# Attention kernel: row scores take every eighth query, and one transfer moves the row maxima into place

## The reference

```python
qkv = jnp.einsum('oc,bchw->bohw', w_qkv, x)          # x is (8, 384, 32, 32)
q, k, v = (to_heads(t) for t in jnp.split(qkv, 3, axis=1))
att = jnp.einsum('bhxd,bhyd->bhxy', q * scale, k)
att = jax.nn.softmax(att, axis=-1)
out = jnp.einsum('bhxy,bhyd->bhxd', att, v)
out = jnp.einsum('oc,bchw->bohw', w_proj, out_as_image) + b_proj[None, :, None, None]
```

## Time and profile before

| | before |
|---|---|
| time, median of 3 runs | 4934.52 us (4933.33 to 4936.31) |
| time of the profiled execution | 4934.93 us |
| its span, first to last instruction | 4933.3 us |
| mean granted clock of TensorE | 0.960 |
| PE busy | 4420.9 us (90%), 14579 matmuls |
| PEld busy | 2648.6 us (54%) |
| DVE busy | 3114.3 us (63%) |
| ACT busy | 2416.2 us (49%) |
| POOL busy | 1192.6 us (24%) |

### The profile page before, as it was taken

One profiled execution on the slowest core, in us unless ns is written; L12 is line 12 of the kernel. 1 busy time (PEld: TensorE's weight loads), 2 busy tenths in 40 slices (PEclk: granted clock), 3 DMA queues, 4 the chain that ended last, 5 costly groups with the idle time before them and its releaser, 6 DMA issues. The chain is left out here.

```text
span 4933.3 us, 48107 instructions
## 1 busy us (share of the span) xinstructions
PE 4420.9 (90%) x14579; PEld 2648.6 (54%) x14579; DVE 3114.3 (63%) x3139; ACT 2416.2 (49%) x3705; POOL 1192.6 (24%) x920
## 2 busy tenths in 40 slices
PE   5999999999999999848999999499399999999999
PEld 4666666666666767623444443388234444444444
DVE  4656666666666666656555554333487788678767
ACT  3757675858585757532222222112154455445544
POOL 2656565555555656400000000111000000000000
PEclk8999999999999999979999999799699999999999
DMA  2010101010101111020011000324200000000000
GB/s 49 21 51 20 50 20 50 20 50 21 47 24 38 33 38 33 28 100 13 39 54 49 39 26 26 103 82 129 109 26 38 38 0 38 38 38 0 38 38 13
DMA packets 62414, 205.55 MB, mean 42 GB/s; under 512 B 32016, under 2 KB 33680, under 8 KB 52496
## 3 DMA queue, kind: packets, MB, share of 16 engines
q1 hardware_dynamic: 56944, 191.90, 11.4%
q0 software_dynamic: 3840, 11.01, 1.0%
q10 hardware_dynamic: 1440, 0.16, 0.0%
HBM read 133.95 MB, written 51.27 MB: 38 GB/s over the span
## 5 line engine op out<-in xcount | busy, mean ns | idle before, releaser
L456 POOL TENSOR_TENSOR probs_lo<-probs,probs_hi 128x512 fp32r<-128x512 f32 x840 | 1116.3, 1351 | 900.7 <-ACT probs L511 889.5
L510 ACT ACTIVATE probs_hi<-s_psum 128x512 fp32r<-128x512 f32 x1024 | 619.0, 605 | 302.7 <-PE s_psum L734 282.9
L2237 PE MATMUL psum<-mixes,conv_t 128*128 128x512 f32 x1728 | 751.1, 592 | 0.0
L581 DVE TENSOR_REDUCE maxima<-m_psum 128x1 fp32r<-128x1024 f32 x520 | 632.1, 1223 | 90.6 <-PE m_psum L712 73.6
L511 ACT ACTIVATE probs<-s_psum 128x512 f32<-128x512 f32 x1024 | 617.9, 603 | 0.0
L2237 PEld LDWEIGHTS psum<-mixes,conv_t 128*128 128x128 f32 x1728 | 327.5, 190 | 409.8 <-issue 409.8
L733 PE MATMUL s_psum<-q_all,k_hi 128*128 128x512 f32 x1026 | 433.6, 423 | 102.7 <-ACT probs L511 102.7
L749 PE MATMUL o_psum<-probs_lo,v 128*112 128x512 f32 x1024 | 410.1, 400 | 17.8 <-DVE probs_lo L652 17.8
L744 PE MATMUL o_psum<-probs_hi,v 128*112 128x512 f32 x1024 | 407.0, 397 | 0.0
L734 PE MATMUL s_psum<-q_all,k_lo 128*128 128x512 f32 x1026 | 404.9, 395 | 0.0
L712 PE MATMUL m_psum<-k_hi,q_all 128*128 128x512 f32 x1040 | 335.9, 405 | 19.8 <-DVE maxima L581 16.2
(11 more groups left out here) (312 smaller groups left out, 7105.2 us busy)
## 6 DMA issues: line engine op xcount, KB each, us to landing
xin<-in_x SPq DMA_DIRECT2D x18, 1536.0 KB, 6.7
xin<-x SPq DMA_DIRECT2D x17, 1536.0 KB, 6.9
xres<-x SPq DMA_DIRECT2D x16, 1536.0 KB, 7.2
k_hi<-k_hi SPq DMA_DIRECT2D x66, 256.0 KB, 3.3
xb<-x SPq DMA_DIRECT2D x4, 4096.0 KB, 16.0
inv_wide<-inv_row SPq DMA_DIRECT2D x64, 192.0 KB, 2.8
x<-xin SPq DMA_DIRECT2D x8, 1536.0 KB, 5.4
x<-xres SPq DMA_DIRECT2D x8, 1536.0 KB, 5.0
```

The source lines that it names most:

```text
L456: pool.tensor_tensor(probs_lo[:, u % RING, :], probs[:, u % RING, :], as_f32(probs_hi[:, u % RING, :]), ALU.subtract).then_inc(pool_low.ne ...
L510: nc.scalar.activation(probs_hi[:, u % RING, :], s_psum[:, u % 2, :], ACT.Exp, scale=SCALE)
L581: nc.vector.tensor_reduce(maxima[:, MAX_ROW + tile:MAX_ROW + tile + 1], slot(tile % 2), AX.X, ALU.max, negate=True).then_inc(rows_max.next ...
L2237: ins = nc.tensor.matmul(bank, conv_w[:, t, down, factor, m * P:(m + 1) * P], mixes[:, factor, t, down:down + S, :].rearrange("p a b -> p ...
```

## The change

The stationary operand of tile `t` of the row scores is no longer 128 consecutive queries, but every eighth query from `t` on (`tile::KEYS`). Then column `t` of `maxima` holds, on partition `p`, the maximum of query `8p + t`, and the 128 x 8 array read partition by partition is the row in its order. One transfer from all of `maxima` to row 48 of `q_all` moves it, 128 pieces of 8 elements. `turn_max`, `copy_max`, the row `max_row`, the float32r identity and their semaphores are gone. What waited for the copy waits for the last maximum (`rows_max`), the row scores of a head wait for the maxima of the head before, and VectorE's first maximum of a head waits for the previous transfer, since `maxima` is now its source.

```diff
@@ -266,10 +266,10 @@
     N = HEADS * UNITS
     RING, SLOTS, LAG = 4, 4, 2
     PAIRS = HEADS // 2
-    ALL_FILLED = 5
+    ALL_FILLED = 4
 
     ROW_UNITS = (2, 3, 4, 5, 6, 7, 8, 9)
-    ROWS_AT, TURN_AT, K_AT, Q_AT = ROW_UNITS[0], 11, 12, 14
+    ROWS_AT, K_AT, Q_AT = ROW_UNITS[0], 12, 14
     GN_AT = HEADS - 5
     USED = 2 * HEAD + 16
     VECTOR_LOWS = [(h, n) for h in range(HEADS) for n in (0, 12, 14) if h > 0 or n > 0]
@@ -321,9 +321,7 @@
         k_hi = sb("k_hi", [P, SLOTS, T], F32R)
         k_lo = sb("k_lo", [P, SLOTS, T], F32R)
         v = sb("v", [P, KEYS, HEADS, USED], F32R)
-        MAX_ROW = 96
-        maxima = sb("maxima", [P, MAX_ROW + KEYS], F32R)
-        max_row = sb("max_row", [P, T], F32R)
+        maxima = sb("maxima", [P, KEYS], F32R)
...
@@ -333,7 +331,6 @@
         inv_cols = sb("inv_cols", [P, KEYS])
         inv_wide = sb("inv_wide", [P, T])
         inv_row = nc.dram_tensor("inv_row", [2, T], F32).ap()
-        ident_r = sb("ident_r", [P, P], F32R)
...
@@ -357,8 +354,6 @@
         qk_low = signal("qk_low", 4 * PAIRS, 4)
         rows_made = signal("rows_made", KEYS * HEADS, KEYS)
         rows_max = signal("rows_max", KEYS * HEADS, KEYS)
-        max_turned = signal("max_turned", HEADS, 1)
-        max_copied = signal("max_copied", HEADS, 1)
...
@@ -388,8 +382,9 @@
         @block.sync
         def _(sp):
             def place_max(g, i):
-                sp.wait_ge(max_copied.sem, max_copied.at(nth(g, 1, i) + 1, i))
-                sp.dma_start(as_f32(q_all[HEAD:HEAD + 1, g % SLOTS, :]), as_f32(max_row[MAX_ROW:MAX_ROW + 1, :])).then_inc(max_placed, 16)
+                sp.wait_ge(rows_max.sem, rows_max.at(nth(g, KEYS, i) + KEYS, i))
+                sp.dma_start(as_f32(q_all[HEAD:HEAD + 1, g % SLOTS, :]).rearrange("a (p j) -> a p j", j=KEYS),
+                             as_f32(maxima[:, :])).then_inc(max_placed, 16)
...
@@ -442,10 +437,9 @@
         @block.gpsimd
         def _(pool):
             pool.memset(as_f32(k_lo[:, :, :]), 0.0).then_inc(filled.next(), 1)
-            pool.memset(as_f32(maxima[:, :]), 0.0).then_inc(filled.next(), 1)
             pool.memset(inv_wide[:, :], 0.0).then_inc(filled.next(), 1)
             pool.memset(as_f32(v[:, :, :, HEAD:64]), 1.0).then_inc(filled.next(), 1)
-            pool.wait_ge(filled.sem, filled.at(4))
+            pool.wait_ge(filled.sem, filled.at(3))
...
@@ -469,13 +463,6 @@
                     target = (k_hi, q_all)[part][0:64, (2 * pair + odd) % SLOTS, :]
                     nc.scalar.copy(target, slot(part)[64 * odd:64 * odd + 64, :]).then_inc(qk_high.next(), 1)
 
-            def copy_max(g, i):
-                at = nth(g, 1, i)
-                act.wait_ge(max_turned.sem, max_turned.at(at + 1, i))
-                if i is not None:
-                    act.wait_ge(max_placed, (i * HEADS + g) * 16)
-                nc.scalar.copy(max_row[MAX_ROW:MAX_ROW + 1, :], slot(0)[MAX_ROW:MAX_ROW + 1, :]).then_inc(max_copied.next(), 1)
...
@@ -494,11 +481,9 @@
                 act.wait_ge(gn_var.sem, gn_var.at(1, i))
                 gn.scalar_rstd(act, act_step, i, gn_rstd)
 
-            nc.scalar.copy(ident_r[:, :], const["ident"]).then_inc(turned_ident.next(), 1)
             group_rstd(None)
             for part in range(2):
                 split(0, part, None)
-            copy_max(0, None)
...
@@ -511,8 +496,6 @@
                         nc.scalar.activation(probs[:, u % RING, :], s_psum[:, u % 2, :], ACT.Exp, scale=SCALE).then_inc(exped.next(), 1)
                         if h % 2 == 0 and n in (K_AT + 1, Q_AT + 1):
                             split(h // 2 + 1, int(n == Q_AT + 1), i)
-                        if n == TURN_AT:
-                            copy_max(h + 1, i)
...
@@ -578,7 +561,9 @@
 
             def row_max(g, tile, i):
                 dve.wait_ge(rows_made.sem, rows_made.at(nth(g, KEYS, i) + tile + 1, i))
-                nc.vector.tensor_reduce(maxima[:, MAX_ROW + tile:MAX_ROW + tile + 1], slot(tile % 2),
+                if tile == 0 and i is not None:
+                    dve.wait_ge(max_placed, (i * HEADS + g) * 16)
+                nc.vector.tensor_reduce(maxima[:, tile:tile + 1], slot(tile % 2),
                                         AX.X, ALU.max, negate=True).then_inc(rows_max.next(), 1)
...
@@ -671,7 +656,6 @@
         def _(pe):
             pe.sem_inc(*weighed.lead())
             pe.wait_ge(filled.sem, filled.at(ALL_FILLED))
-            pe.wait_ge(turned_ident.sem, turned_ident.at(1))
...
@@ -706,20 +690,13 @@
                     pair = nth(g // 2, 1, i)
                     pe.wait_ge(qk_low.sem, qk_low.at(4 * pair + 4, i))
                     pe.wait_ge(k_again, 32 * (g // 2 + 1) + (0 if i is None else i * (32 * PAIRS)))
-                if tile >= 2:
+                if tile >= 2 or g > 0:
                     pe.wait_ge(rows_max.sem, rows_max.at(nth(g, KEYS, i) + tile - 1, i))
                 for half in range(2):
                     ins = nc.tensor.matmul(m_psum[:, 2 * (tile % 2) + half, :],
-                                           q_all[:, g % SLOTS, tile * P:(tile + 1) * P],
+                                           q_all[:, g % SLOTS, tile::KEYS],
                                            k_hi[:, g % SLOTS, half * HALF:(half + 1) * HALF], start=True, stop=True)
                 ins.then_inc(rows_made.next(), 1)
-
-            def turn_max(g, i):
-                pe.wait_ge(rows_max.sem, rows_max.at(nth(g, KEYS, i) + KEYS, i))
-                for tile in range(KEYS):
-                    ins = nc.tensor.matmul(m_psum[0:MAX_ROW + 1, tile // 4, (tile % 4) * P:(tile % 4 + 1) * P],
-                                           maxima[:, tile:tile + MAX_ROW + 1], ident_r[:, :], start=True, stop=True)
-                ins.then_inc(max_turned.next(), 1)
...
@@ -755,8 +732,7 @@
             project_qk(0, 1, None)
             for tile in range(KEYS):
                 row_scores(0, tile, None)
-            turn_max(0, None)
-            pe.wait_ge(max_copied.sem, max_copied.at(1))
+            pe.wait_ge(rows_max.sem, rows_max.at(KEYS))
             values(None)
...
@@ -766,13 +742,9 @@
                     if n in ROW_UNITS:
                         if n == ROWS_AT and h == 0:
                             pe.wait_ge(y_made.sem, y_made.at(0, i))
-                        if n == ROWS_AT and h % 2 == 0:
-                            pe.wait_ge(max_copied.sem, max_copied.at(h, i))
                         row_scores(h + 1, ROW_UNITS.index(n), i)
-                    if n == TURN_AT:
-                        turn_max(h + 1, i)
                     if h % 2 == 0 and n == K_AT:
-                        pe.wait_ge(max_copied.sem, max_copied.at(h + 1, i))
+                        pe.wait_ge(rows_max.sem, rows_max.at(KEYS * (h + 1), i))
                         if h == HEADS - 2:
                             pe.wait_ge(xn_ready.sem, xn_ready.at(CT, i))
                         project_qk(h // 2 + 1, 0, i)
@@ -781,12 +753,13 @@
                     if h % 2 == 0 and n == Q_AT:
                         project_qk(h // 2 + 1, 1, i)
                     if h == GN_AT + 1 and n == UNITS - 5:
+                        pe.wait_ge(rows_max.sem, rows_max.at(KEYS * (h + 1), i))
                         groups(i)
                     scores(u + LAG, i)
                     if u > 0:
                         weigh(u - 1, i)
                 weigh(N - 1, i)
-                pe.wait_ge(max_copied.sem, max_copied.at(HEADS, i))
+                pe.wait_ge(rows_max.sem, rows_max.at(KEYS * HEADS, i))
                 values(i)
```

More of the change, by code:

```diff
@@ L374, in attention_layer @@
         filled = signal("filled")
-        turned_ident = signal("turned_ident")
         def slot(n):
@@ L523, in _ @@
                 keep_values(i)
-            for s in (act_step, gn_rstd, v_kept, qk_high, max_copied, exped, o_copied):
+            for s in (act_step, gn_rstd, v_kept, qk_high, exped, o_copied):
                 s.end_of_pass()
@@ L810, in _ @@
                     project_out(n, 0, PAIRS)
-            for s in (gn_groups, v_made, qk_made, rows_made, max_turned, scored, weighed, projected):
+            for s in (gn_groups, v_made, qk_made, rows_made, scored, weighed, projected):
                 s.end_of_pass()
```

## The result

The changed kernel takes 4860.1 us, median of 4 runs (4856.3 to 4864.2); beside them the kernel before took 4933.9 us, median of 4. The ratio is 0.985, with a 95% interval of 0.9833 to 0.9867: 74 us faster. The same file, timed again among the last experiments, took 4870.0 us (4863.7 to 4882.7), ratio 0.9871 (0.9853 to 0.989). All eight times together have their middle at 4863.9 and a spread of 26 us, where all those of the kernel before lie within 7 us. Where part of that spread comes from is one of the things the experiments showed. The profiled execution has a span of 4857.6 us, before 4933.3.

The account below looks back on a forecast made before the run. Attention loop paced by TensorE in row-score units, ScalarE's exponentials in others, TensorE's projections in even heads. Savings of 9.3 us an image, 74 for eight, plus 2.0 before the loop: 4934.5 - 76 = 4858 us, range 4840 to 4880.

Parts of the forecast that it names:

- Odd heads: Heads 1 and 3: without turning and copy, ScalarE starts unit 12 at 643.09 instead of 644.95, saving 1.86 us each.
- Even heads: TensorE's k projection no longer waits for turning and copy, starting at 613.69 instead of 614.72: 1.0 us saved each.
- The strided weight load: Row-score loads of columns 8 elements apart hide under the 0.23 us matmul pace: nothing; other bound 1,024 x 9 ns.
- rival C: The strided load outgrows its cover in row-score units: +205 us, 5063 us; decides from 0.075 us over; chance 0.05.
- the wrong row: The last layer's turning of `conv_rows`, step 27, 0.1165 us a pair: read as a step adding some 9 ns a load.
- Head 7: The maxima's transfer still lands behind the residual load, so next scores start at 311.7: 0.75 us saved, ends 0.2 and 1.86.
- Heads 5 and 6: Head 5: VectorE's full queue leaves 0.8 us, ends 0.2 and 1.86; head 6: TensorE's projection gains 1.0 us.
- Before the loop: Values start earlier without the turning and the 1.09 us wait for the copy: 2.7 us, taken as 2.0.
- The sum: One image: even heads 4.0, heads 1 and 3 3.7, head 5 0.8, head 7 0.75, together 9.3 us.
- D: Rival for the whole kernel: the work removed was hidden anyway, 4934 us; chance 0.03.
- A: Rival: nothing collides, heads 5 and 7 give 1.86 us each, 94 us in all, 4840 us; chance 0.08.
- B: Rival: heads 5 and 7 give nothing and 9 ns a load show everywhere: 54 us, 4880 us; chance 0.14.

Follow-up runs that it names:

- contiguous loads: Changed kernel with row-score tiles of 128 consecutive queries again, the transfer as it is: 4856.6 us, ratio 0.9844.
- put-back kernels: Changed kernel with the eight turning matmuls put back, 4887.2 us, or with ScalarE's copy put back, 4902.1 us; nobody waits for either.
- three pairs of kernels: Step 8 against contiguous: in the kernel before (4943.8, 4934.6 us), with the transfer first in head 7 (4853.3, 4844.5), and in the change (4860.1 or 4863.9, 4856.6).
- step 2: Changed kernel with every second query of a quarter, four transfers, issued before the residual load in head 7: 4847.1 us, ratio 0.9826.
- step 4: Changed kernel with every fourth query of a half, two transfers: 4876.4 us; with these also before the residual load in head 7, 4851.1 us.
- place-first kernel: Changed kernel with the maxima's transfer issued before the residual load in head 7: 4853.3 us, ratio 0.9835.

## Why the prediction was right, point by point

The forecast of 4858 us stands against 4860.1 (4870.0 the second time), both inside the range. Its mechanism was the right one; several terms were off and partly cancelled (the load's cost against head 6's gain), which was luck, and one was a mean over something that varies.

- **Odd heads, 1.86 us each.** Right. With contiguous loads heads 1 and 3 are 1.85 and 1.90 shorter than before; in the change 1.70 and 1.67, because the step takes 0.2 back. The two put-back kernels show that both parts, turning and copy, were exposed.
- **Even heads, 1.0 us each.** Right for heads 0, 2 and 4: 0.99, 1.04 and 0.86 with contiguous loads, 0.74, 0.89 and 0.59 in the change. The turning alone is 0.65 to 0.74 of it.
- **The strided weight load, taken at 0 with 9.4 us as the other bound.** This is the step that failed: the term was mis-sized. It costs 0.21 us a head, 13 us in the loop; the medians of three pairs of kernels with and without it are 9, 9 and 4 to 7 us apart, with head 5's swings in them. The price came from a turning, which pays 1 ns for a step where a matmul pays 133 (0.240 - 0.107 us). It stayed small only because a matmul of 512 columns covers nearly all of it: about 245 ns from start to start where it was 232, 0.013 us over the cover, where rival C decides from 0.075. But the load was 2.2 times the contiguous one, not far from the 2.8 at which C decides; C's chance of 0.05 leaned on the wrong row.
- **Head 7, 0.75 us.** The mechanism was right: the maxima land with the residual load, and scores wait for a DMA. From the load's issue to the scores it was 312.15 - 304.54 = 7.61 us and is 302.04 - 294.89 = 7.15, so 0.46 where 0.45 was worked out. The images without a second half-clock stretch average 38.38 us, 0.59 less than before. The mean saved only 0.16, since in one image of seven the longer wait and the stretch together took 3 us; in the second profile the head was even 0.26 longer. The prediction knew the stretch of head 5, but not that the wait it forecast here could bring a second one.
- **Heads 5 and 6, 0.8 and 1.0 us.** Together they saved 3.2 in one profile and 2.3 in the other, against 1.8. Head 6 saved 1.87 both times (2.12 with contiguous loads), 0.9 more than forecast: by the put-back kernels the copy alone is worth 1.13 of it, so the forecast was wrong to give ScalarE's share nothing there. Head 5 saved 1.33 or 0.44 in the mean, but 0.15 to 0.2 with the half-clock stretch in the same place: the 0.8 was too much, the prediction's lower end of 0.2 was nearer, and the rest is where the stretch fell. That VectorE's queue takes the gain back, as the prediction thought it might, fits this and was not tested.
- **Before the loop, 2.0 us.** The values start at 82.56 where they stood at 85.15, 2.6 us earlier. The loop's first exponential is 3.2 us earlier in one profile and 1.8 in the other.
- **The sum.** An image at contiguous loads is 9.83 us shorter against the 9.3 forecast, so the parts without the load were under-sized by 0.5: head 6 by 1.1, against 0.5 too much in head 5. The load took 1.7 an image, of which head 5 gave back 1.0 in the first profile by where its stretch fell.

Of the rivals, D (hidden anyway) and A (nothing collides) are out: the load does collide. B had the right costs, the step and little gain in heads 5 and 7, but each at a different size.

The Trainium skill (SBUF — State Buffer, section on the DMA port swizzle) did speak of this cost: each access to a new 16-byte line pays. These runs agree with it at a step of 32 bytes, 325 ns against 193, and against the prediction's row. They differ at the step that the same section calls free: 4 fp32 elements apart the load is recorded at 310 ns, and only 2 apart at 193. The same page of the Trainium skill asks in its table (section Specifications) for at least two hits on a line for full bandwidth; by that rule step 2 is free and step 4 is not, and that is what the records show. No run timed a load at step 2 or 4 without cover.

## What to carry to other kernels

Price a new access pattern by the same kind of instruction: a turning is no stand-in for a matmul's load. A stationary operand with a step is affordable as long as the matmul covers it; here a step of two fp32 elements was free within 3 us, and cutting the index into quarters of step 2 kept the layout trick without the price. Before a small transfer on which the next work depends is issued behind a large load on the same queue, try it ahead of the load: here that was one moved line, and it was worth 7 to 11 us, 25 at step 4, and the extra half-clock stretches.

When single heads or images of one profiled execution differ, profile the same file again before their differences are read as effects of an edit.

## What the runs showed of the hardware

A small transfer issued 2.2 us behind a load of 1.5 MB landed 4.3 to 6.6 us after its own issue: in 13 of the 16 images of two executions within 0.4 us of that load's landing, in three 1.2 to 1.6 us behind it; issued ahead of that load it took 1.9 (place-first kernel). The load record of a stationary operand is not its cost: under the same 0.23 us of cover 311 ns at step 4 cost 5.6 us in the loop where 325 at step 8 cost 12.7, and under 0.43 us of cover (plain float32, 512 moving columns) step 8 cost nothing. Ten waits of TensorE of 2.0 to 3.2 us for a transfer (four in the change, six at step 4) each went with 3.4 us or more at the 1.2 GHz level; head 7 of such an image of the change was 2.6 to 3.1 us longer, with the longer wait in it. What starts the half-clock stretch inside head 5, which stands behind a wait of 1.8 us, and why it has just these places, stays open.
